# Low parts of one weight matrix by accumulating transfers, and the second tile's convolution in other banks

## The reference

```
scores = y @ Wr.T                       # 64 experts
gates  = softmax of the 16 largest, zero elsewhere
h      = einsum('nd,krd->nkr', y, A)    # 64 experts x 16 = 1024 columns
out    = x + 2 * einsum('nkr,kdr->nd', h * gates, B)
```

## Time and profile before

| what | value |
|---|---|
| median of 3 runs | 894.25 us (894.18 to 894.29) |
| the profiled execution's own time | 894.25 us |
| its span, first to last instruction | 892.5 us |
| TensorE busy | 879.5 us (99%) |
| VectorE busy | 753.8 us (84%) |
| ScalarE busy | 376.1 us (42%) |
| GpSimd busy | 6.5 us (1%) |
| transfers | 103.32 MB, mean 116 GB/s |

### The profile page before, as it was taken

One profiled execution on the slowest core, in us unless ns is written; L12 is line 12 of the kernel. 1 busy time (PEld: TensorE's weight loads), 2 busy tenths in 40 slices (PEclk: granted clock), 3 DMA queues, 4 the chain that ended last, 5 costly groups with the idle time before them and its releaser, 6 DMA issues.

```text
span 892.5 us, 15771 instructions
## 1 busy us (share of the span) xinstructions
PE 879.5 (99%) x4478; PEld 781.4 (88%) x4478; DVE 753.8 (84%) x2597; ACT 376.1 (42%) x642; POOL 6.5 (1%) x22
## 2 busy tenths in 40 slices
PE   5999999999999999999999999999999999999998
PEld 3667999998889998889999889999889999889997
DVE  8989998988889888889888889888889888888722
ACT  5763563444444344444344444334444334442100
POOL 2000000000000000000000000000000000000000
PEclk9999999999999999999999999999999999999999
DMA  7721315444333444333444434444333445333331
GB/s 238 241 57 47 77 33 141 141 118 121 115 120 108 124 118 126 115 119 111 118 118 131 113 117 110 118 118 137 110 116 108 118 118 141 111 114 114 93 95 48
DMA packets 74759, 103.32 MB, mean 116 GB/s; under 512 B 23972, under 2 KB 56804, under 8 KB 74740
## 3 DMA queue, kind: packets, MB, share of 16 engines
q1 hardware_dynamic: 74212, 102.63, 40.2%
q0 software_dynamic: 160, 0.10, 0.2%
q10 hardware_dynamic: 368, 0.36, 0.1%
HBM read 67.34 MB, written 34.93 MB: 115 GB/s over the span
## 4 chain that ended last, share of the span: by engine, by line
PE 95%; DVE 3%; ACT 1%; issue 0%; DMA 0%; ACTq 0%; DVEq 0%
PE out_ps L1432 26%; PE h_ps L1432 19%; PE out_ps L1436 13%; PE h_ps L1436 9%; PE turn_ps L1432 8%; PE turn_ps L1436 4%; PE conv_ps L1388 2%; PE conv_ps L1389 2%; PE conv_ps L1390 2%; PE conv_ps L1361 1%; PE conv_ps L1398 1%; PE conv_ps L1362 1%; PE conv_ps L1399 1%; PE conv_ps L1400 1%; PE conv_ps L1363 1%; PE h_ps L1441 1%
## 5 line engine op out<-in xcount | busy, mean ns | idle before, releaser
L1432 PE MATMUL out_ps<-b_lo,g_hi 128*128 128x512 f32 x496 | 196.1, 395 | 0.0
L1432 PE MATMUL out_ps<-b_hi,g_hi 128*128 128x512 f32 x496 | 194.7, 393 | 0.3 <-ACT g_hi L584 0.3
L1432 PE MATMUL h_ps<-a_hi,y_hi 128*128 128x384 f32 x480 | 161.4, 336 | 0.0
L1432 PE MATMUL h_ps<-a_lo,y_hi 128*128 128x384 f32 x480 | 161.3, 336 | 0.0
L1436 PE MATMUL out_ps<-b_hi,g_lo 128*128 128x512 f32 x496 | 122.6, 389 | 0.0
L1432 PEld LDWEIGHTS out_ps<-b_lo,g_hi 128*128 128x128 f32 x496 | 93.2, 188 | 21.2
L1432 PEld LDWEIGHTS out_ps<-b_hi,g_hi 128*128 128x128 f32 x496 | 93.0, 188 | 20.4 <-ACT g_hi L584 0.9
L1436 PEld LDWEIGHTS out_ps<-b_hi,g_lo 128*128 128x128 f32 x496 | 93.0, 188 | 20.0
L857 DVE SCALAR_TENSOR_TENSOR z<-swapped,step_other,part 128x64 f32<-128x64 f32 x384 | 92.3, 282 | 11.9
L850 DVE SCALAR_TENSOR_TENSOR part<-z,step_own,conv_ps 128x64 f32<-128x64 f32 x384 | 90.5, 277 | 8.7 <-ACT z L486 0.4
L1436 PE MATMUL h_ps<-a_hi,y_lo 128*128 128x384 f32 x480 | 93.1, 336 | 0.0
(11 more groups left out here) (244 smaller groups left out, 1480.7 us busy)
## 6 DMA issues: line engine op xcount, KB each, us to landing
xt_in<-in_xt SPq DMA_DIRECT2D x32, 512.0 KB, 3.3
x_in<-in_x SPq DMA_DIRECT2D x62, 256.0 KB, 3.7
out<-x_in SPq DMA_DIRECT2D x62, 256.0 KB, 3.1
moved<-square_sb SPq DMA_DIRECT2D x28, 512.0 KB, 2.7
square_sb<-moved SPq DMA_DIRECT2D x112, 128.0 KB, 2.9
b_in<-in_b_t SPq DMA_DIRECT2D x8, 512.0 KB, 7.8
a_in<-in_a_t SPq DMA_DIRECT2D x8, 512.0 KB, 9.1
moved_in<-square_in SPq DMA_DIRECT2D x26, 128.0 KB, 2.8
```

Source lines behind the costliest of these rows:

```text
L1432: pe.matmul(o, hi[:, c, :], moving[:, c, columns], start=first and c == order[0] and moving is w_hi, stop=False)
```

## The change

The low parts of `a` are no longer made by VectorE. ScalarE writes minus the high part over `a_in` (an activation with scale -1 that rounds to float32r, `minus_high`), and GpSimd issues a transfer that reads `a` from memory again and adds it to what stands there. The third of columns 0 to 383 is so made before the second tile's projection up reaches it, so this third becomes split; the high parts for it are made earlier (`high_last`). The second tile's convolution goes to `h_ps`, its turned powers and kernel row (`turn_in(2)`, `kernel_row(2)`) to `turn_ps`, and the orders of TensorE, ScalarE and VectorE around it change. `y_hi` and `y_lo` of the second tile are made too, so their counts move by one tile. The core of the diff:

```diff
+        conv_1 = [h_ps[:, i, :] for i in range(HT)]
+        in_ps_2 = turn_ps[:, 0, 0:HT * P].rearrange("p (h s) -> p h s", h=HT)
+        k_ps_2 = turn_ps[:, 1, 0:HT * P].rearrange("p (h s) -> p h s", h=HT)
@@ GpSimd, behind its last transfer
+            pool.wait_ge(s_minus_hi, 1)
+            pool.dma_start(a_lo[:, :, 0:384], a_t[:, :, 0:384], accum_op=ALU.add).then_inc(s_alo[2], 16)
+            pool.wait_ge(s_minus_hi, 2)
+            pool.dma_start(a_lo[:, :, 768:ER], a_t[:, :, 768:ER], accum_op=ALU.add).then_inc(s_alo[0], 16)
+            pool.dma_start(a_lo[:, :, ER:EW], wr_t, accum_op=ALU.add).then_inc(s_alo[0], 16)
+            pool.wait_ge(s_minus_hi, 3)
+            pool.dma_start(a_lo[:, :, 384:768], a_t[:, :, 384:768], accum_op=ALU.add).then_inc(s_alo[1], 16)
@@ ScalarE
+            def high_last():
+                for i in LATE[5:]:
+                    act.wait_ge(s_w[i], 16)
+                act.activation(a_hi[:, NC // 2:NC, 0:384], a_in[:, NC // 2:NC, 0:384], ACT.Copy).then_inc(s_hilast, 1)
+            def split_rest(i):
+                _, arrived, hi, _ = loads[i]
+                act.activation(hi[:, 384:ER], arrived[:, 384:ER], ACT.Copy).then_inc(s_whi, 1)
+            def minus_high(n, up_before, highs):
+                _, c0, width, _ = H_PARTS[n]
+                act.wait_ge(s_up, up_before)
+                act.wait_ge(s_hilast, 1)
+                act.wait_ge(s_whi, highs)
+                act.activation(a_lo[:, :, c0:c0 + width], a_in[:, :, c0:c0 + width], ACT.Copy, scale=-1.0).then_inc(s_minus_hi, 1)
@@ ScalarE, first_step
                 decays(2)
+                high_last()
+                minus_high(2, 3, len(HIGH) - 4)
                 sines(2)
+                high_x(2)
                 other_products(2)
                 high_out(2)
-                high_in(2)
-                high_x(2)
+                high_in(2, in_ps_2)
                 theta(3)
-                copy_k(2)
+                copy_k(2, k_ps_2)
                 first_copies(2)
+                for i in range(HT):
+                    high_y(1, i)
                 tables(3)
                 for i in LATE[5:]:
-                    split_weights(i)
+                    split_rest(i)
@@ ScalarE, second_step
                 high_z(2)
+                minus_high(0, 4, len(HIGH))
                 high_turned(1, 0, 2, g_hi)
...
                 high_x(3)
+                minus_high(1, 5, len(HIGH))
                 copy_k(3)
@@ VectorE, first_step
                 arguments(2)
-                scale_of(0)
-                add_rows(0, 0)
-                make_powers(2)
-                out_factors(2)
-                for i in range(HT):
-                    mask_y(1, i)
-                low_out(2)
-                low_in(2)
-                low_x(2)
-                arguments(3)
-                add_skip(2)
+                mask_y(1, 0, conv_1)
+                make_powers(2)
+                low_x(2)
+                out_factors(2)
+                low_out(2)
+                low_in(2, in_ps_2)
+                mask_y(1, 1, conv_1)
+                arguments(3)
+                add_skip(2)
+                scale_of(0)
+                add_rows(0, 0)
                 add_rows(0, 1)
@@ VectorE, second_step: low_up(0), low_up(1), low_up(2) go
                 gate(1)
+                for i in range(HT):
+                    low_y(1, i)
                 states(2, range(MIDDLE, FED))
@@ TensorE, up and first_step
-                    if first:
-                        pe.wait_ge(s_wlo, len(MIDST) + n + 1)
+                    if first and n < 2:
+                        pe.wait_ge(s_whi, len(HIGH))
+                        pe.wait_ge(s_alo[n], 16 * (2 - n))
...
                 down_high(0, (0, 1, 2, 3))
+                whole_near_1()
                 pe.wait_ge(s_glo, 2)
                 down_low(0)
-                whole_conv(1)
-                turn_in(2)
+                whole_from_states_1()
                 down_high(1, (0, 1, 2, 3))
+                turn_in(2, in_ps_2)
                 down_low(1)
-                kernel_row(2)
+                kernel_row(2, k_ps_2)
                 feed(2)
@@ TensorE, second_step
-                for n in range(len(H_PARTS)):
+                for n in range(2):
                     for c in range(NC):
                         last = whole_product(n, c)
                     last.then_inc(s_up, 1)
+                o, c0, width, _ = H_PARTS[2]
+                pe.wait_ge(s_yhi, HT)
+                pe.wait_ge(s_alo[2], 16)
+                product_high(o, y_hi, a_hi, a_lo, slice(c0, c0 + width), range(NC), first=True)
+                pe.wait_ge(s_ylo, HT)
+                product_low(o, y_lo, a_hi, slice(c0, c0 + width), range(NC)).then_inc(s_up, 1)
```

More of the change, by code:

```diff
@@ L207, in build @@
         s_whi, s_wlo = sem("s_whi"), sem("s_wlo")
+        s_hilast, s_minus_hi, s_alo = sem("s_hilast"), sem("s_minus_hi"), [sem(f"s_alo_{n}") for n in range(3)]
         s_theta, s_whole, s_args, s_sine, s_decay, s_powers, s_other, s_raw = (
@@ L508, in high_moved_in, with high_in @@
                                square_in[:, :].rearrange("p (q h x) -> p h q x", q=JM, h=HT), ACT.Copy).then_inc(s_inhi, 1)
-            def high_in(t):
+            def high_in(t, source=in_ps):
                 act.wait_ge(s_turned, t + 1)
-                act.activation(in_hi[:, :, :], in_ps, ACT.Copy).then_inc(s_inhi, 1)
+                act.activation(in_hi[:, :, :], source, ACT.Copy).then_inc(s_inhi, 1)
             def whole_in(t, source):
@@ L814, in low_moved_in, with low_in @@
                                   op=ALU.subtract).then_inc(s_inlo, 1)
-            def low_in(t):
+            def low_in(t, source=in_ps):
                 dve.wait_ge(s_inhi, t + 1)
-                dve.tensor_tensor(out=in_lo[:, :, :], in0=in_ps, in1=in_hi[:, :, :].bitcast(F32), op=ALU.subtract).then_inc(s_inlo, 1)
+                dve.tensor_tensor(out=in_lo[:, :, :], in0=source, in1=in_hi[:, :, :].bitcast(F32), op=ALU.subtract).then_inc(s_inlo, 1)
             def add_skip(t):
@@ L862, in low_z, with mask_y @@
                 dve.tensor_tensor(out=z_lo[:, :, :, :], in0=z[:, :, :, :], in1=z_hi[:, :, :, :].bitcast(F32), op=ALU.subtract).then_inc(s_zlo, 1)
-            def mask_y(t, i):
+            def mask_y(t, i, conv=conv_ps):
                 dve.wait_ge(s_conv, HT * t + i + 1)
-                dve.tensor_tensor(out=y_m[:, :, i * B:(i + 1) * B], in0=conv_ps[i][:, :].rearrange("p (c b) -> p c b", b=B),
+                dve.tensor_tensor(out=y_m[:, :, i * B:(i + 1) * B], in0=conv[i][:, :].rearrange("p (c b) -> p c b", b=B),
                                   in1=mask[:, :, :], op=ALU.mult).then_inc(s_ym, 1)
@@ L878, in low_y @@
                 head = slice(i * B, (i + 1) * B)
-                dve.wait_ge(s_yhi, HT * (t - EXACT) + i + 1)
+                dve.wait_ge(s_yhi, HT * (t + 1 - EXACT) + i + 1)
                 dve.tensor_tensor(out=y_lo[:, :, head], in0=y_m[:, :, head], in1=y_hi[:, :, head].bitcast(F32),
                                   op=ALU.subtract).then_inc(s_ylo, 1)
[L883 to L890, removed]
             def low_weights(i):
@@ L1180, in second_step @@
                 gate_part(1, 0)
-                low_up(0)
+                gate_part(1, 1)
                 low_near(2)
-                gate_part(1, 1)
                 low_z(2)
@@ L1194, in second_step @@
                 low_in(3)
-                low_up(1)
                 for i in range(HT):
@@ L1198, in second_step @@
                 low_x(3)
-                low_up(2)
                 scale_of(1)
@@ L1343, in turn_in, with kernel_row @@
                 last.then_inc(s_turned, 1)
-            def kernel_row(t):
+            def kernel_row(t, target=k_ps):
                 pe.wait_ge(s_olo, t + 1 - EXACT)
-                pe.matmul(k_ps, real[:, :], o_hi[:, :, 0:P], start=True, stop=False)
-                pe.matmul(k_ps, real[:, :], o_lo[:, :, 0:P], start=False, stop=True).then_inc(s_kps, 1)
+                pe.matmul(target, real[:, :], o_hi[:, :, 0:P], start=True, stop=False)
+                pe.matmul(target, real[:, :], o_lo[:, :, 0:P], start=False, stop=True).then_inc(s_kps, 1)
             def whole_row(t, target):
@@ L1357, in feed @@
                 pe.wait_ge(s_xlo, t + 1 - EXACT)
-                pe.wait_ge(s_ym, HT * t)
+                if not (isinstance(t, int) and t == EXACT):
+                    pe.wait_ge(s_ym, HT * t)
                 for i in range(HT):
@@ L1416, in whole_from_states_0, with whole_near_1, whole_from_states_1 @@
                               skip_group_check=True).then_inc(s_conv0 if n == 0 else s_conv, 1)
-            def whole_conv(t):
-                pe.wait_ge(s_t, HT * 16 * t)
-                pe.wait_ge(s_part, HT * (FED - 1) * (t + 1))
+            def whole_near_1():
+                pe.wait_ge(s_t, HT * 16)
                 for i in range(HT):
```

(13 more changed lines are left out.)

## The result

The changed kernel takes 901.41 us (median of 6 runs, 900.91 to 902.06) against 894.2 us on the same chip: the ratio is 1.0081, 95% interval 1.0068 to 1.0094. That is 7.2 us slower. I had forecast 893.4 and a range to 898.5, so the time lies outside it, on the side of rival B and beyond B's own 897.4.

The account below looks back on a forecast made before the run. TensorE, busy 99% of the span, was taken to bound the kernel. Minus 0.97, minus 0.73 and plus 0.85 gave minus 0.85, 893.4 us; range 892.1 to 898.5, the forecast's own 892.6 to 894.6.

Parts of the forecast that it names:

- rival B: Last accumulate with read, read and write in turn, 13.9 us, holds up `up(2)`: plus 3.15, 897.4 us; chance 0.22.
- part 5: Accumulating transfers: the last, taken as 9.9 us, lands late for the second part of `up(2)`: plus 0.85 us.
- The halved rate: Accumulating transfers: the second read takes the engine's time again, so the last needs 2.0 + 7.9 = 9.9 us.
- The estimate of 9.2 us: Last transfer priced by the skill's two sections: lands at 91.7, whole sum minus 1.55 us.
- rival A: All accumulating transfers land in time, an accumulate taking 9 us or less: minus 1.70, 892.55 us; chance 0.30.
- Part 1: Second tile's last third of the projection up, from whole float32 to three split products: minus 0.97 us.
- Part 2: Second tile's convolution in `h_ps`, ahead of `down_low(0)`: second step starts at 58.21 instead of 58.94, minus 0.73 us.
- The chain to `copy_k(2)`: Ahead of the second step: x's load through `copy_k(2)` ends at 58.1, TensorE comes at 58.2; 0.1 us to spare.
- Rival C: First accumulate slows the load of x for the third tile, second step late: minus 0.3, 893.9 us; chance 0.14.
- Part 3: ScalarE's new work, `high_last`, `minus_high` and `high_y(1)`, is hidden in idle time or offset: nothing.
- Part 4: VectorE: three `low_up` go, two `low_y(1)` come; `gate_part(1, 2)` at about 73.2, ahead of TensorE's need: nothing.

Follow-up runs that it names:

- experiment 7: Transfers alone, one at a time, no reference computation; 1.57 MB in rows of 1536 B: plain load 7.8 us (SyncE), 8.5 (GpSimd), accumulating 11.6 and 11.7.
- experiment 5: Changed kernel with SyncE's transfers held back until the last accumulate has landed: 897.96 us, ratio 1.0035 to the kernel before.
- experiment 3: Changed kernel with 24 extra matmuls, results unused, ahead of TensorE's wait for the last transfer: 899.02 us, ratio 1.0048 to the kernel before.
- experiment 1: Kernel before plus only the convolution in `h_ps` and the new orders; VectorE makes all low parts, second tile whole: 894.78 us against 894.39.
- experiment 8: Banks-only kernel, but low parts of columns 768 to 1087 by ScalarE's negation and accumulating transfers: 894.43 us against 894.39 for the kernel before.
- experiments 2: Changed kernel without the last transfer, VectorE making the low part of columns 384 to 767: 893.16 us against 894.39 for the kernel before.
- experiment 6: Changed kernel with `minus_high(0)` ahead of `high_z(2)` and `minus_high(1)` right behind it, so transfers issue earlier: 893.18 us against 894.49 for the kernel before.

## Why the prediction was wrong

**The step that failed is the length of the last accumulating transfer in part 5.** I put 9.9 us; it takes 15.3. The place and the two dates were right: issue at 82.35 against 82.5 predicted, wanted at 91.58 against 91.55. So a hole of 0.85 us became a lateness of 6.16. Of the 5.4 us that were missing in the transfer, 1.8 are its own (11.7 alone, experiment 7) and 3.1 are SyncE's traffic (experiment 5). The last 0.5, the difference between 11.7 alone and 12.2, is not settled; the second pair was still on its way when the last transfer was issued, which no experiment takes away. The halved rate was right: 205 GB/s against the 199 that I used. What I undervalued in the own part is the share that is not movement, 2.0 us taken from a load of 128 long rows by SyncE, against 3.9. The number of rows explains little of that: with 384 rows of 4096 B the accumulate took 10.9 us, 0.7 less. What makes up the rest is open.

The Trainium skill's Collectives: The Full Stack, section "The bandwidth ceiling: the fold count and why AG ≠ RS ≠ AR", says of the reducing step of collectives between cores that its two source reads halve the rate. The trace agrees for an accumulate inside one core: 205 GB/s against 376 for the plain load in experiment 7. The estimate of 9.2 us, which also used the fit in the Trainium skill's DMA: Bandwidth & Descriptors, section "Anatomy of one DMA — SWDGE (gpsimd) path", did not hold: 11.6 measured.

**The traffic beside it** I had named in rival A and then given no time, and in rival B I said the opposite, that nothing else wants the engines. Both could be summed from the code: the Toeplitz loads and the store move up because VectorE is free and TensorE earlier.

**What no case had is the clock.** I priced lateness one for one. A lateness of 6.16 us cost 9.1, and behind the idle 2.96 us of experiment 5 the clock fell to 0.50 as well. Of the 8.3 us between my minus 0.85 and the 7.44 seen, 5.3 are the longer transfer and 2.9 the clock. With it, a transfer of 15.3 us gives minus 1.67 plus 6.16 plus 2.9, the 7.4 us seen; without it, 898.7, which is near the top of my range and is what experiment 3 measured (899.0).

**Part 1** was minus 0.89 instead of minus 0.97, by the two thirds together (9.43 against 10.32). **Part 2** gives a second step that starts 0.96 us earlier; but the projection down ahead of the changed stretch already started 0.15 earlier (43.56 against 43.71), behind a shorter wait for a weight load. So the change's own part is minus 0.81, against my minus 0.73; experiment 1, where that start is 43.69, has minus 0.77. With 0.18 us lost in small pieces elsewhere this gives 1.67 of lead against my 1.70: the sum agrees better than its terms, and 0.15 of it is chance. **The chain to `copy_k(2)`** was 0.3 us shorter than I had it. ScalarE's timeline after:

```profile
46.58 2.77 ACT L485 ACTIVATE a_lo<-a_in 128x3072 fp32r<-128x3072 f32 x1
...
57.47 0.36 ACT L560 ACTIVATE k_sb<-turn_ps 128x256 f32<-128x256 f32 x1
...
79.30 2.76 ACT L485 ACTIVATE a_lo<-a_in 128x3072 fp32r<-128x3072 f32 x1
```

`copy_k(2)` starts at 57.47, where I had 57.75. Rival C did not happen: the first accumulate did not slow x, which ScalarE took at 52.44, 3.2 us behind its issue at 49.23. **Part 3** held: `minus_high(2)` ends at 49.35, and TensorE waits for nothing behind it. **Part 4** was right that VectorE's freed time wins nothing by itself, and incomplete: in experiment 1, without it, the banks' 0.8 us were lost again at the gated part. By the traces the two parts of the change need each other; the time of experiment 8 does not confirm it.

**Rival A** is what experiments 2 and 6 are: 893.2, 1.2 to 1.3 us below the kernel before. I had 1.70. **Rival B** named the right side, at 897.4, but with read, read and write in turn, which would move about 133 GB/s where 205 were measured; its "3072 short rows" don't fit the 1024 rows of part 5 either.

## What to carry to other kernels

When work moves from an engine to a transfer, put its date of issue, its length and the date of need in one line, and take the length with the traffic that is beside it then: here 11.7 us alone, 15.3 in company, 9 available. On a kernel whose TensorE is always busy, count a late operand for more than its lateness when that is some microseconds: behind idle stretches of 3.0, 5.8 and 6.0 us the clock fell here, and 1.6 to 2.9 us were lost on top. See whether an engine idles earlier in its queue, as ScalarE did ahead of `high_z(2)`: moving the issue there won 8.2 us here, holding other traffic back 3.4.

## What the runs showed of the hardware that I had not expected

- An idle TensorE of 3.0 us (experiment 5) is followed by a granted clock of 0.50, as one of 6.0 us is; the extra matmuls of experiment 3, with 0.6 us of idle time behind them, kept it at 1.00.
- An accumulate of 1.57 MB from GpSimd takes 11.6 us alone against 8.5 for the same plain load, and is nearly as long with rows of 4096 B (10.9) as with rows of 1536 B.
- Accumulates close together do not gain from each other: in experiment 6 the one issued at 75.0, behind a pair that landed at 83.0, took 15.6 us, 7.6 of them behind that landing.
